# A batch's steps dealt out anew over five engines, and softmax's reductions folded

## The chip, the cores and the metric

One core of a Trainium2 chip runs the kernel; the others are idle. The time is the device time of one execution in microseconds. A core has TensorE (PE), VectorE (DVE), ScalarE (ACT) and GpSimd (POOL), each with a queue of its own that it works off in order, and SyncE (SP), which here only issues DMAs. Engines wait for each other through semaphores.

## What is computed

The input x is 4 batches of 1024 tokens with 128 channels, float32. Two blocks follow one another, each between two layer norms:

```python
x = x + layernorm(attention(layernorm(x)))
x = x + layernorm(experts(layernorm(x)))
```

Attention (8 heads of 16 channels) scores each token against 11 earlier positions: itself and those 1, 2, 4, ... 512 back. Over these 11 scores goes a softmax, whose weights sum the values at the same positions. Added to it are a causal convolution of the values over 7 taps per channel, and a linear attention (elu(q)+1, elu(k)+1) over all tokens. The sum goes through Wo, and attention adds its own input. The second block has 8 experts of 128 to 64 to 128 with gelu, of which a sigmoid gate keeps the best two per token, and a shared expert of the same size.

## The kernel before

It is a software pipeline written out by hand: each engine's program is a list of steps in a loop `for b in range(B + 1)`. In turn b the attention of batch b runs together with the experts of batch b-1, which has two units of 512 tokens, u0 = 2b-2 and u1 = 2b-1. `more` means that a batch b+1 follows, `ffn` that a batch b-1 exists. The turn ends with the keys, queries and values of batch b+1. Turn 0 has no experts, turn 4 has only experts. In the text batch b is the turn b.

The steps, in the order in which a batch needs them (lines of the profile):

- **Scores.** DVE multiplies queries with shifted keys in three groups of 4, 4 and 3 products (`products`, L957, L283), PE sums over each head's channels in three groups (`sum_heads`, L1330), ACT copies them (`scores`), PE turns them to token-major (`turn_scores`, L1260). `linear_state` on PE (L1311) and DVE (L975 to L981) makes fk^T v; the third score group waits for its `kv_ready`.
- **Softmax** on DVE: `softmax_logits` (L983) adds a mask, takes the maximum over the 12 slots and subtracts it; ACT takes exponentials (`exponentials`, L698); `softmax_weights` (L1001) sums them, takes the reciprocal (`rden`) and scales. The twelfth slot, masked out, is then given 1/z of the linear part, from `zden`. `weigh_low` (L1010) scales with it what PE made in `low` (L1348).
- **Terms.** For each of 8 tiles of 128 tokens DVE weighs the 11 shifted value tiles (`weigh`, L1032), PE sums them in PSUM by transposes (`sum_terms`, L1362), DVE adds the convolution (`add_conv`, L1052), PE applies Wo and adds the block's input (`output`, L1372). The shifted values `v_shift` are copies made by 18 DMAs of SP from token-major v (`shift_v`, L369 to L372).
- **Convolution.** ACT scales v by one tap at a time (`scale_taps`, L666), each into a home of its own (`tap_home`: convT, tapT0 to tapT2, then the buffers kexp and qexp, and tapT0 again). POOL adds them by six accumulating DMAs (`sum_taps_first`, `_second`, `_third`, L503); it waits for the landing of one before it issues the next of the same target. `key_parts` of the next batch waits for the last.
- **Layer norms.** ACT squares with a sum (`norm2`, `norm3_squares`, `norm4`), POOL takes the power -0.5 (`ln1` to `ln4`, L482 and L484), ACT or DVE applies it (`normalise1`, `normalise3`, `residual`, `finish`, `scale_outputs`).
- **Experts**, per unit: `turn_x3` (PE), `evacuate_x3` (ACT), `gate_logits` (PE: a matmul into the front bank C4, which holds logits and the shared expert's hidden part; ACT: its copy to `gate_shared`, and the exponential gexp), `turn_logits` (PE); 24 small dependent steps `gates` on DVE, each waiting for the one before; `gates_expert_major` (PE, ACT), `gate_rows`; `hidden` (PE matmuls, ACT gelu, 4 chunks); `spread_gates` (PE), `gate_hidden` (DVE, L1145); `experts_out` (PE, L1465, 4 tiles of 10 matmul records). DVE does u0's gates ahead of softmax_logits and u1's among the term tiles 0 to 3.
- **Fillers.** `keep_busy` (L1474) issues transposes of the identity into a free bank. Their result is not used. Before: 12 ahead of the third score group, 10 ahead of `turn_x3` of u0, 4 and 8 around u1's logits, per batch, and further ones in turns 0 and 4.

ACT needs another function table for gelu than for exp; changing costs an ACT_TABLE_LOAD.

The projections of batch b+1 stand on PE as `project_k` ahead of the terms, `project_q` at tile 1 and `project_v` at tile 5, before and after the change.

## Time and profile before

| | |
|---|---|
| median of 3 runs | 298.2 us (297.54 to 298.52) |
| the profiled execution's own time | 298.78 us |
| its span in the trace | 296.9 us |
| PE busy | 255.2 us, 86% |
| DVE busy | 233.1 us, 79% |
| ACT busy | 198.8 us, 67% |
| POOL busy | 87.1 us, 29% |
| chain that ended last | PE 53%, ACT 19%, DVE 16%, POOL 7% |
| mean granted clock of TensorE | 0.974 |

Busy time is the time in which at least one instruction of the engine runs; register, semaphore and DMA-issuing instructions aren't counted. The chain is followed back from the last instruction, at each step to what released it. The granted clock is 1.00 where TensorE runs at 2.4 GHz and 0.50 where it runs at 1.2.

### The profile page before, as it was taken

To read this page: it belongs to the slowest core of one execution; us is meant where nothing else is said; L and a number is where in the kernel's file an instruction comes from. 1 tells how busy PE (TensorE), PEld (TensorE's weight loads), DVE (VectorE), ACT (ScalarE), POOL (GpSimd) and SP (SyncE) were. 2 spreads that over 40 slices of the span, in tenths; PEclk is the share of its full clock that TensorE was granted. 3 is DMA by queue.
4 is the path that set the end of the run, shared out by engine and by line. 5 is a ranking of instruction groups with operands and counts; after the bars stand their busy time and mean duration, and the time that the engine had idled before them with its cause. 6 is when DMAs were issued, how large, how long until landed. Compare 5 with 4: busy or idle time off the path is not lost.

```text
span 296.9 us, 4821 instructions
## 1 busy us (share of the span) xinstructions
PE 255.2 (86%) x1665; PEld 180.1 (61%) x1665; DVE 233.1 (79%) x574; ACT 198.8 (67%) x461; POOL 87.1 (29%) x152
## 2 busy tenths in 40 slices
PE   5965987896599899989898899989898699699893
...
GB/s 198 128 45 243 227 191 191 95 0 111 234 243 201 153 44 2 141 0 162 242 235 223 162 2 35 35 26 221 238 220 219 97 2 71 2 1 1 0 14 94
DMA packets 24258, 35.27 MB, mean 119 GB/s; under 512 B 4053, under 2 KB 17198, under 8 KB 24234
## 3 DMA queue, kind: packets, MB, share of 16 engines
...
q0 software_dynamic: 3888, 13.37, 25.0%
...
q14 instruction: 11, 0.09, 0.1%
...
## 4 chain that ended last, share of the span: by engine, by line
PE 53%; ACT 19%; DVE 16%; POOL 7%; issue 4%; POOLq 0%; DVEq 0%; ACTq 0%
PE psH L1362 7%; PE psY L1465 6%; PE psA L1330 4%; PE psF L1427 4%; DVE prods L283 3%; PE psA L1268 3%; ACT xn L604 3%; PE psA L1260 3%; PE psG L1465 3%; PE psY L1311 3%; PE psA L1465 3%; DVE hid L1145 3%; POOL rstd L484 2%; PE psF L1402 2%; ACT xn L724 2%
## 5 line engine op out<-in xcount | busy, mean ns | idle before, releaser
L283 DVE TENSOR_TENSOR prods<-qT,kT 128x1024 f32<-128x1024 f32 (+1 forms) x48 | 50.4, 1106 | 2.8 <-POOL neg_half L447 2.8
L482 POOL TENSOR_SCALAR var<-ss 128x4 f32<-128x4 f32 (+1 forms) x25 | 12.5, 502 | 111.5 <-ACT squares L770 55.8
L1362 PE MATMUL psH<-ident,prods 128*128 128x128 f32 x324 | 40.0, 273 | 0.0
L1362 PEld LDWEIGHTS psH<-ident,prods 128*128 128x128 f32 x324 | 36.4, 141 | 2.3 <-issue 2.3
L1032 DVE TENSOR_TENSOR prods<-v_shift,prob 128x896 f32<-128x896 f32 x32 | 34.6, 1083 | 0.0
L484 POOL TENSOR_TENSOR rstd<-var,neg_half 128x4 f32<-128x4 f32 (+2 forms) x28 | 33.0, 1180 | 2.3
L1145 DVE TENSOR_TENSOR hid<-hid,psG 128x512 f32<-128x512 f32 x32 | 20.8, 682 | 15.8 <-PE psG L1451 15.2
L1427 PE MATMUL psF<-x3T,w 128*128 128x512 f32 x58 | 29.0, 610 | 0.4 <-ACT gexp L738 0.3
L1330 PE MATMUL psA<-prods,slot_sel 128*32 128x512 f32 x168 | 24.1, 624 | 4.1 <-DVE prods L283 4.1
L1032 DVE TENSOR_TENSOR prods<-v_tok,prob 128x128 f32<-128x128 f32 (+2 forms) x60 | 20.8, 371 | 1.9 <-PE psH L1362 1.9
L1465 PEld LDWEIGHTS psY<-w,hid 128*128 128x128 f32 x140 | 17.4, 206 | 5.7 <-DVE prods L1016 5.7
L1465 PE MATMUL psY<-w,hid 128*128 128x128 f32 x140 | 18.1, 292 | 3.2 <-DVE prods L1016 3.2
L503 POOL DMA_DIRECT2D convT<-tapT x9 | 8.1, 902 | 40.4 <-DMA convT<-tapT 22.4
L1474 PE MATMUL psG<-ident 128*128 128x128 f32 x126 | 17.1, 296 | 3.1 <-POOL ident L414 3.1
L1268 PE MATMUL psA<-xnT,wqkv 128*128 128x512 f32 x36 | 18.1, 631 | 1.5 <-ACT xnT L593 1.5
L746 ACT ACTIVATE hid<-psF,b1c 128x512 f32<-128x512 f32 x29 | 18.7, 684 | 0.7 <-PE psF L1427 0.5
L1474 PEld LDWEIGHTS psG<-ident 128*128 128x128 f32 x126 | 16.0, 154 | 5.2 <-POOL ident L414 3.1
L1427 PEld LDWEIGHTS psF<-x3T,w 128*128 128x128 f32 x58 | 9.7, 189 | 12.5 <-issue 8.5
L770 ACT ACTIVATE squares<-psY 128x128 f32<-128x128 f32 x14 | 3.7, 278 | 16.2 <-PE psY L1465 16.2
L1330 PEld LDWEIGHTS psA<-prods,slot_sel 128*32 128x32 f32 x168 | 5.2, 113 | 13.7 <-issue 11.4
L666 ACT ACTIVATE tapT<-vT,cw 128x1024 f32<-128x1024 f32 x12 | 13.1, 1139 | 0.0
L1359 PE MATMUL psH<-ident,prods 128*128 128x128 f32 x32 | 9.1, 285 | 3.5 <-DVE prods L1052 2.5
...
## 6 DMA issues: line engine op xcount, KB each, us to landing
...
convT<-tapT POOLq DMA_DIRECT2D x11, 512.0 KB, 5.0
x_res<-L_attn_x SPq DMA_DIRECT2D x4, 512.0 KB, 9.9
tapT<-tapT POOLq DMA_DIRECT2D x4, 512.0 KB, 10.1
...
x_in<-L_attn_x SPq DMA_DIRECT2D x3, 512.0 KB, 4.2
...
convT<-kexp POOLq DMA_DIRECT2D x3, 512.0 KB, 7.4
```

Of the source, the lines that this page charges most:

```text
L283: return eng.tensor_tensor(prods[:, QUADS * (s % 2) + q, t0:t1], qT[:, t0:t1], kT[:, PRE - off + t0:PRE - off + t1], ALU.mult)
L484: return nc.gpsimd.tensor_tensor(rstd[:, cols], var[:, cols], neg_half[:, cols], ALU.pow)
L666: nc.scalar.activation(tap_home(b, tap), vT[:, VPRE - tap:VPRE - tap + T], ACT.Copy, scale=cw[:, TAPS - 1 - tap:TAPS - tap]).then_inc(tap_ ...
L746: nc.scalar.activation(hid[:, c, half_cols(u)], hidden_bank(u, c), ACT.Gelu, bias=b1c[:, c:c + 1]).then_inc(hidden_free, 1)
L1032: return nc.vector.tensor_tensor(dst, src.rearrange("p m (h d) -> p m h d", d=HD), w, ALU.mult)
L1145: nc.vector.tensor_tensor(hid[:, c, cols], hid[:, c, cols], psG[:, c % 2, :], ALU.mult).then_inc(gated, 1)
L1268: pe.matmul(psA[:, half, :], wqkv[:, bass.ts(part, P)], xnT[(b + 1) % 2][:, bass.ts(half, HALF)], start=True, stop=True).then_inc(psA_full, 1)
L1330: ins = pe.matmul(psA[32 * q:32 * q + 32, half, :], ksum_sel[:] if low else slot_sel[:, s, :], fqT[:, cols] if low else prods[:, QUADS * ( ...
L1362: ins = pe.matmul(dst, terms[:, j % TERM_BUFS, m, :], ident[:], is_transpose=True, start=False, stop=(m == live[-1]))
L1427: pe.matmul(hidden_bank(u, c), w1[:, bass.ts(c, P)], x3T[:, half_cols(u)], start=True, stop=True).then_inc(hidden_full, 1)
L1465: ins = pe.matmul(output_tile(u, n), hid[:, c, bass.ts(j, P)], w2[:, c, :], start=(c == CH - 1), stop=(c == CH - 2))
L1474: pe.transpose(bank[:, bass.ts(k % TPH, P)], ident[:], ident[:])
```

## The change

- **Fold.** `over_terms` takes the place of both `tensor_reduce`: it halves the 12 slots to 6, these to 3, and combines those three in two steps, four chained tensor_tensor operations. `softmax_chain` counts 11 steps in place of 5. The reciprocal of zden is now taken in `weigh_low`, in place, and no longer stored in prob.
- **DVE order.** `stats` behind the second product group; `finish` and `residual(u1)` behind `linear_state`; two gate steps of u0 ride with the third group, two with `linear_state`; `weigh_low` and half of u0's `gate_hidden` ahead of `softmax_weights`; u1's gates ride with tiles 1 to 4, its `gate_hidden` at tiles 6 and 7.
- **Unit 2b's front.** `turn_x3`, `gate_logits` and their copies go from the start of turn b+1 to the end of turn b. On ACT the copy of C4 is split off as `evacuate_shared`.
- **Tap 6** has the home fkT and waits for the token-major fk in place of the first tap sum; taps 4 and 5 are scaled at the turn's start, tap 6 among u1's front.
- **POOL order.** `ln1`, `ln4`, the first tap sums (before: at the end of the turn before), `ln3(u1)`, the other tap sums; `ln2` of the second unit at the turn's end.
- **PE order.** `experts_out(u0)` is cut in three around u1's logits, `experts_out(u1)` in three around the token-major turns. The fillers of the steady turns are gone; the last attention turn has two of 10.

The diff, without its unchanged context where that says nothing ("..." stands for lines left out; indentation is cut per piece):

```diff
-FILL_SUM = 12
 FILL_FRONT = 5
-FILL_X3, FILL_C4, FILL_LOGITS = 10, 4, 8
+FILL_LAST = 10
...
-return (convT[b % 2], tapT[0], tapT[1], tapT[2], kexp, qexp, tapT[0])[tap][:]
+return (convT[b % 2], tapT[0], tapT[1], tapT[2], kexp, qexp, fkT)[tap][:]
...
-if ffn:
-    ln2(u1)
-if 2 <= b < B:
-    ln4(u0 - 1)
-if attn and b:
-    sum_taps_second(b)
-if more:
-    ln1(b + 1)
-if ffn and attn:
-    ln3(u1)
-if attn and b:
-    sum_taps_third(b)
-if ffn and attn:
-    ln4(u0)
-    add_residual(u0)
-if b == 0:
-    first_conv_sums()
 if attn:
+    if more:
+        ln1(b + 1)
+    if b >= 2:
+        ln4(u0 - 1)
+    if b:
+        sum_taps_first(b)
+        ln3(u1)
+        sum_taps_second(b)
+        sum_taps_third(b)
+        ln4(u0)
+        add_residual(u0)
+    else:
+        first_conv_sums()
     ln2(2 * b)
-if more:
-    sum_taps_first(b + 1)
-if attn:
     ln3(2 * b)
-if not attn:
+    ln2(2 * b + 1)
...
-act.wait_ge(sums_added, N_DMA * upto(b - 1, N_SUMS, 1))
+act.wait_ge(psA_full, filled(b, PSA_FK_TOK, 1))
...
-def gate_logits(u):
+def evacuate_shared(u):
     act.wait_ge(front_full, upto(u, N_FRONT, 2))
     copy(gate_shared[:, half_cols(u)], front(u, C4)).then_inc(front_free, 1)
+def gate_logits(u):
...
-    evacuate_x3(u0)
-if ffn:
     gate_logits(u0)
-if b:
-    scale_taps(b, range(5, TAPS))
-if ffn:
+    scale_taps(b, range(4, 6))
+    if more:
+        normalise1(b + 1, range(0, TPH))
     norm3_squares(u1)
-    hidden(u0, range(0, 2))
-if more and b:
-    normalise1(b + 1, range(0, TPH))
 scores(b)
 if b == 0:
     scale_first_taps(range(4, TAPS))
-if more and b:
-    normalise1(b + 1, range(TPH, NT))
 if ffn:
-    normalise3(u1)
+    if more:
+        normalise1(b + 1, range(TPH, NT))
+    hidden(u0, range(0, 2))
+    gates_expert_major(u0)
+    gate_rows(u0)
     hidden(u0, range(2, 4))
     shared_hidden(u0)
-    gates_expert_major(u0)
-    gate_rows(u0)
-    evacuate_x3(u1)
 exponentials(b)
-if ffn:
-    gate_logits(u1)
 if b == 0:
     normalise1(b + 1)
 if more:
     evacuate_x(b + 1)
+if ffn:
+    normalise3(u1)
+    evacuate_x3(u1)
+    scale_taps(b, range(6, TAPS))
+    evacuate_shared(u1)
+    gate_logits(u1)
+if more:
     evacuate_k(b + 1)
 if ffn:
     hidden(u1, range(0, 2))
-if ffn:
     norm4(u0)
 if more:
     evacuate_q(b + 1)
 if ffn:
     scale_outputs(u0)
-if ffn:
     hidden(u1, range(2, 4))
     shared_hidden(u1)
     gates_expert_major(u1)
 if more:
     key_parts(b + 1)
     query_parts(b + 1)
-norm2(2 * b)
-if not more:
+    norm2(2 * b)
+    evacuate_v(b + 1)
+    scale_taps(b + 1, range(0, 1))
+    norm3_squares(2 * b)
+    norm2(2 * b + 1)
+    normalise3(2 * b)
+    token_major_v(b + 1)
+    evacuate_x3(2 * b)
+    scale_taps(b + 1, range(1, 2))
+    token_major_fk(b + 1)
+    evacuate_shared(2 * b)
+    scale_taps(b + 1, range(2, 3))
+    if ffn:
+        norm4(u1)
+    scale_taps(b + 1, range(3, 4))
+else:
+    norm2(2 * b)
     norm3_squares(2 * b)
     nc.scalar.activation(table_load[:], neg_half[:, 0:1], ACT.Exp)
     norm2(2 * b + 1)
     normalise3(2 * b)
-if more:
-    evacuate_v(b + 1)
-    scale_taps(b + 1, range(0, 4))
-if more:
-    token_major_v(b + 1)
-    token_major_fk(b + 1)
-    norm3_squares(2 * b)
-    norm2(2 * b + 1)
-    scale_taps(b + 1, range(4, 5))
-    normalise3(2 * b)
-    if ffn:
-        norm4(u1)
...
+def over_terms(op, into):
+    tt, n = nc.vector.tensor_tensor, NM // 4
+    softmax_chain(tt(folded[:], prob[:, :, 0:NM // 2, :], prob[:, :, NM // 2:NM, :], op))
+    softmax_chain(tt(folded[:, :, 0:n, :], folded[:, :, 0:n, :], folded[:, :, n:2 * n, :], op))
+    softmax_chain(tt(into[:], folded[:, :, 0, :], folded[:, :, 1, :], op))
+    softmax_chain(tt(into[:], into[:], folded[:, :, 2, :], op))
...
-softmax_chain(nc.vector.tensor_reduce(top[:], prob[:].rearrange("p j m h -> p j h m"), AX_X, ALU.max))
+over_terms(ALU.max, top)
 nc.vector.tensor_tensor(prob[:], prob[:], top[:].unsqueeze(2).to_broadcast([P, NT, NM, HEADS]),
...
-    softmax_chain(nc.vector.tensor_reduce(den[:], prob[:].rearrange("p j m h -> p j h m"), AX_X, ALU.add))
-    softmax_chain(nc.vector.reciprocal(rden[:], den[:]))
+    over_terms(ALU.add, den)
+    softmax_chain(nc.vector.reciprocal(den[:], den[:]))
     softmax_chain(nc.vector.tensor_tensor(prob[:], prob[:],
-                                          rden[:].unsqueeze(2).to_broadcast([P, NT, NM, HEADS]),
+                                          den[:].unsqueeze(2).to_broadcast([P, NT, NM, HEADS]),
                                           ALU.mult))
-    softmax_chain(nc.vector.reciprocal(prob[:, :, M_LOW, :], zden[:]))
 def weigh_low(b):
+    softmax_chain(nc.vector.reciprocal(zden[:], zden[:]))
     dve.wait_ge(low_ready, upto(b, 1, 1))
     for half, src in enumerate((psH, psY)):
         tiles = slice(half * TPH, (half + 1) * TPH)
-        w = prob[:, tiles, M_LOW, :].unsqueeze(3).to_broadcast([P, TPH, HEADS, HD])
+        w = zden[:, tiles, :].unsqueeze(3).to_broadcast([P, TPH, HEADS, HD])
         ins = nc.vector.tensor_tensor(low_terms[:, tiles].rearrange("p j (h d) -> p j h d", d=HD),
...
+if u % 2 == 0 or u == 2 * B - 1:
...
         products(b, 1)
         key_features(0)
     query_features(b)
-    if more and b:
-        stats(b + 1)
     if b:
         products(b, 1)
-def gate_step_of(u, first):
-    def beside(n):
-        if attn and ffn:
-            gates(u, (first + n,))
-    return beside
-if attn and not more:
-    products(b, 2)
-if attn and b >= 2:
-    finish(u0 - 1)
-if ffn:
-    residual(u1)
-if more:
-    products(b, 2, gate_step_of(u0, 0))
-if attn:
-    linear_state(b, gate_step_of(u0, 3 if more else 0))
+        if more:
+            stats(b + 1)
+    products(b, 2, range(0, 1))
+    products(b, 2, range(1, 3), gate_step_of(u0, 0))
+    linear_state(b, gate_step_of(u0, 2))
     if b == 0:
         stats(b + 1)
         centre_weights()
         dve.wait_ge(consts_ready, 2)
+    if b >= 2:
+        finish(u0 - 1)
     if ffn:
-        gates(u0, range(5 if more else 2, 24))
+        residual(u1)
+        gates(u0, range(4, 24))
     softmax_logits(b)
     if ffn:
-        gate_hidden(u0, range(0, 4))
+        gate_hidden(u0, range(0, 2))
+    weigh_low(b)
+    if ffn:
+        gate_hidden(u0, range(2, 4))
     softmax_weights(b)
-    weigh_low(b)
     for j in range(NT):
         def two_gate_steps(n):
-            if ffn and j < TPH:
-                gates(u1, range(2 * (3 * j + n), 2 * (3 * j + n + 1)))
+            if ffn and 1 <= j <= TPH:
+                gates(u1, range(2 * (3 * (j - 1) + n), 2 * (3 * (j - 1) + n + 1)))
         weigh(b, j, two_gate_steps)
         if ffn:
-            if j in (5, 7):
-                gate_hidden(u1, range(j - 5, j - 3))
+            if j in (6, 7):
+                gate_hidden(u1, range(2 * (j - 6), 2 * (j - 5)))
...
-if 0 < u < 2 * B - 2 and u % 2 == 0:
-    keep_busy(FILL_X3, front(u, X3))
...
-if u < 2 * B - 2 and u % 2:
-    keep_busy(FILL_C4, front(u, C4))
...
-if u < 2 * B - 2 and u % 2:
-    keep_busy(FILL_LOGITS, front(u, LOGITS))
...
-    turn_x3(u0)
-    gate_logits(u0)
+    turn_logits(u0)
 linear_state(b, b == 0)
-if ffn:
-    turn_logits(u0)
 if b:
     sum_heads(b, 1)
+else:
+    keep_busy(FIRST_FILL_SUM, psG[:, 1, :])
+sum_heads(b, 2)
 if ffn:
     hidden(u0, range(0, 2))
-keep_busy(FILL_SUM if b else FIRST_FILL_SUM, psG[:, 1, :])
-sum_heads(b, 2)
-if ffn:
-    hidden(u0, (2,))
 turn_scores(b)
 if ffn:
-    hidden(u0, (3,))
+    gates_expert_major(u0)
 low(b)
 if b == 0:
     pe.wait_ge(w_centred, 1)
+    keep_busy(FIRST_FILL_X, psG[:, 1, :])
+if ffn:
+    hidden(u0, (2,))
+    spread_gates(u0, range(0, 2))
+    hidden(u0, (3,))
+if more:
+    turn_x(b + 1)
+if not more:
+    pe.wait_ge(scores_read, 2 * B)
+    keep_busy(FILL_LAST, psA[:, 0, :])
+if ffn:
+    spread_gates(u0, range(2, 4))
+if more:
+    project_k(b + 1)
+else:
...
 if ffn:
     turn_x3(u1)
-    gates_expert_major(u0)
-if b == 0:
-    keep_busy(FIRST_FILL_X, psG[:, 1, :])
-if more:
-    turn_x(b + 1)
-if ffn:
-    spread_gates(u0, range(0, 2))
+    experts_out(u0, (0,))
     gate_logits(u1)
-    spread_gates(u0, range(2, 4))
+    experts_out(u0, (1,))
     turn_logits(u1)
-if more:
-    project_k(b + 1)
-if ffn:
+    experts_out(u0, range(2, TPH))
     hidden(u1, range(0, 2))
 if b == 0:
     project_q(b + 1)
-if ffn:
-    experts_out(u0)
-if b == 0:
...
-            spread_gates(u1, range(2 * (j - 5), 2 * (j - 4)))
-    if more:
-        if j == 1 and b:
-            project_q(b + 1)
-        if j == 5:
-            project_v(b + 1)
+        if j in (5, 7):
+            spread_gates(u1, range(j - 5, j - 3))
+    if more and j == 1 and b:
+        project_q(b + 1)
+    if more and j == 5:
+        project_v(b + 1)
     sum_terms(b, j)
     if j == TPH:
         output(b, 0)
 output(b, 1)
 if more:
+    if ffn:
+        experts_out(u1, range(0, 2))
     token_major_v(b + 1)
+    turn_x3(2 * b)
+    if ffn:
+        experts_out(u1, range(2, 3))
     token_major_fk(b + 1)
+    gate_logits(2 * b)
 if ffn:
-    experts_out(u1, range(TPH if more else TPH - 1))
+    experts_out(u1, range(TPH - 1, TPH) if more else range(TPH - 1))
```

## Rows read from the trace of the kernel before

**Rows 1.** Busy time by stretch, halves A and B of batches 1, 2, 3 (in turn).

Columns: stretch, its length, busy time (and instructions) of PE, weight loads, DVE, ACT, POOL, granted clock of TensorE, DMA share, GB/s.

```profile
69.22:94.06 24.84, 19.16 (x121) 11.12 (x120) 21.02 (x61) 18.20 (x50) 9.91 (x16) 0.93 0.91 218
94.06:133.22 39.16, 36.27 (x234) 26.10 (x233) 33.01 (x75) 31.30 (x62) 6.64 (x7) 1.00 0.35 76
133.22:158.21 24.99, 22.92 (x171) 15.39 (x170) 22.12 (x65) 19.73 (x59) 14.79 (x19) 1.00 0.87 209
158.21:197.37 39.16, 36.28 (x234) 26.11 (x233) 33.03 (x75) 31.29 (x62) 5.95 (x7) 1.00 0.34 74
197.37:221.19 23.82, 22.64 (x171) 15.44 (x170) 20.18 (x49) 18.76 (x56) 12.48 (x14) 1.00 0.88 205
221.19:258.03 36.84, 30.51 (x205) 23.42 (x203) 31.88 (x72) 17.13 (x46) 5.62 (x7) 0.95 0.39 88
```

**Rows 2.** Groups by line and shape, PE, batch 2 (134.34 to 198.49): filler transposes.

```profile
L1474 PE MATMUL psF<-ident 128*128 128x128 f32 x22 | 3.1, 280 | 0.0
...
L1474 PE MATMUL psG<-ident 128*128 128x128 f32 x12 | 1.5, 272 | 0.0
```

**Rows 3.** Waits of DVE, batch 2: half A, then half B.

```profile
DVE y_out L1155 <- POOL rstd L484: 1.2, 1, 1.2
...
DVE hid L1145 <- PE psG L1451: 4.2, 3, 1.7
DVE prods L1052 <- PE psH L1362: 1.2, 1, 1.2
```

**Rows 4.** Timeline of DVE, batch 2: logits start, weighing starts, first add_conv.

```profile
158.21 0.22 DVE L988 TENSOR_SCALAR zden<-psA 128x64 f32<-128x64 f32 x1 [0.88 <-PE psA L1260]
...
171.84 0.28 DVE L1032 TENSOR_TENSOR prods<-v_tok,prob 128x128 f32<-128x128 f32 x1
...
184.66 0.69 DVE L1052 TENSOR_TENSOR prods<-psH,convT 128x512 f32<-128x512 f32 x1 [1.25 <-PE psH L1362]
```

**Rows 5.** Groups by line and shape, DVE, batch 2.

```profile
L283 DVE TENSOR_TENSOR prods<-qT,kT 128x1024 f32<-128x1024 f32 x11 | 12.9, 1213 | 0.0
...
L1003 DVE TENSOR_REDUCE den<-prob 128x64 f32<-128x768 f32 x1 | 1.5, 1520 | 0.0
...
L1005 DVE TENSOR_TENSOR prob<-prob,rden 128x768 f32<-128x768 f32 x1 | 1.0, 957 | 0.0
...
L990 DVE TENSOR_TENSOR prob<-psA,mask 128x384 f32<-128x384 f32 x2 | 1.0, 547 | 0.0
...
L1096 DVE TENSOR_TENSOR gtmp<-gtmp,first_pref 128x32 f32<-128x32 f32 x2 | 0.4, 192 | 0.1
```

**Rows 6.** Groups by line and shape, ACT, batch 2: softmax's exponentials.

```profile
L698 ACT ACT_TABLE_LOAD x1 | 1.3, 1283 | 0.0
...
L698 ACT ACTIVATE prob<-prob 128x768 f32<-128x768 f32 x1 | 0.8, 844 | 0.0
```

**Rows 7.** Busy time by stretch, batch 3, around the start of experts_out.

```profile
232.00:233.00 1.00, 0.00 (x0) 0.00 (x0) 0.93 (x3) 0.24 (x1) 0.00 (x0) 1.00 1.02 205
...
235.00:236.00 1.00, 1.00 (x7) 1.00 (x7) 0.97 (x3) 0.00 (x0) 0.00 (x0) 0.50 0.00 0
```

**Rows 8.** Timeline of PE: experts_out of the first unit, batches 2 and 3.

```profile
171.98 4.73 PE L1465 MATMUL psY<-w,hid 128*128 128x128 f32 x40 [0.22 <-DVE prods L1016]
...
234.12 6.19 PE L1465 MATMUL psY<-w,hid 128*128 128x128 f32 x40 [2.78 <-DVE prods L1016]
```

**Rows 9.** Timeline of POOL, batch 2: tap sums issued.

```profile
133.90 0.93 POOL L503 DMA_DIRECT2D convT<-tapT  x1 [3.56 <-ACT tapT L666]
...
149.72 0.93 POOL L503 DMA_DIRECT2D convT<-kexp  x1 [3.38 <-ACT qexp L666]
...
157.52 0.93 POOL L503 DMA_DIRECT2D convT<-tapT  x1 [1.01 <-DMA convT<-kexp]
...
166.37 0.86 POOL L503 DMA_DIRECT2D convT<-tapT  x1 [7.92 <-DMA convT<-tapT]
```

**Rows 10.** Page, DMA issues: KB each, median us from issue to landing.

```profile
convT<-tapT POOLq DMA_DIRECT2D x11, 512.0 KB, 5.0
```

More of the change, by code:

```diff
@@ L955, in query_features, with products @@
                                                op1=ALU.add).then_inc(fq_ready, 1)
-            def products(b, s, beside=lambda n: None):
+            def products(b, s, some=range(QUADS), beside=lambda n: None):
                 if s == 0 and b:
@@ L969, in products @@
                     dve.wait_ge(psA_free, first_count(PSA_Q, 1))
-                for n, q in enumerate(mine):
+                for n, q in enumerate(mine[some.start:some.stop]):
                     ins = product(nc.vector, s, q, HALF if b == 0 and s == 0 else 0, T)
@@ L1164, in _, with gate_step_of, beside @@
                 u0, u1 = 2 * b - 2, 2 * b - 1
+                def gate_step_of(u, first):
+                    def beside(n):
+                        if ffn and n >= 0:
+                            gates(u, (first + n,))
+                    return beside
                 if attn:
```

11 lines of the change are left out of this document (7 added, 4 removed).

## The prediction

> **What bounds the kernel now.** I read three views. First the page's busy shares and the chain that ended last: TensorE (PE) is busy 86% of the span, VectorE (DVE) 79%, ScalarE (ACT) 67%, and the chain changes engines all the time. No engine is full, so handovers are the price. Second, DVE's own list of instructions, from which I took two marks in each batch: k, where `key_features` ends and the products start, and L, where `softmax_logits` starts. They cut batches 1, 2 and 3 into halves A (k to L) and B (L to the next k; in batch 3 to the end of the last `add_conv`). In [rows 1] the reader sees each half's length and DVE's busy time in it. The six halves are 188.8 us, and DVE works 161.2 us of them: at most 27.6 us can be won without taking work from DVE. PE is busy 167.8 us, but part of that is filler: 22 and 12 transposes of `keep_busy` in one batch, 280 and 272 ns each as records overlap, at a start-to-start of about 0.11 us, so some 4 us a batch [rows 2]. Without it PE has about 156 us of work, less than DVE. So the engine to watch is DVE, and the question for every part is which wait of DVE goes and which comes. Third, DVE's waits in batch 2: in A it waits 1.2 us for `ln4` in `finish` [rows 3] and 0.9 us for the turned scores, at L itself [rows 4]; in B 4.2 us for the spread gates and 1.2 us for the terms' sums [rows 3]. In the other batches the sets are alike.
>
> **Half A, part by part.**
> - ACT and PE now turn x3, project C4 and copy it (`turn_x3`, `gate_logits`, `evacuate_x3`, `evacuate_shared` of unit 2b) at the end of the batch before, among `experts_out(u1)`. It is the same work; what leaves A is a ping-pong between PE and ACT ahead of the logits of unit u0. It costs something on the other side: `token_major_v` on ACT now stands behind `normalise3(2b)`, and that behind POOL's `ln3`; v_tok and fk_tok come some 2 and 3 us later after k than before. They feed the v_shift copies, `linear_state` and the first score sums. I cost this at nothing, because DVE has eight products (1.2 us each, the next starting a little before one ends [rows 5]) and the query features to do in that time.
> - `finish(u0-1)` and `residual(u1)` go from ahead of the third product group to behind `linear_state`. POOL now takes `ln1(b+1)` before `ln4`; `ln1` waits for `stats`, which moved behind the second products. I get `ln4` ready about when DVE arrives, and keep 0.2 us of wait in batch 2. The 0.9 to 2.8 us wait for the turned scores goes: the scores are summed while DVE does finish, residual and 20 gate steps (each one starts 0.224 us after the last).
> - So DVE runs A nearly without a wait. Its busy time [rows 1] plus the gaps between the dependent gate steps (about 0.035 each, 0.8 in all) gives 21.0 + 1.1 = 22.1, 22.1 + 1.1 = 23.2, and 20.2 + 0.7 = 20.9 us, against 24.8, 25.0 and 23.8: 7.4 us less.
>
> **Half B, part by part.**
> - The folds: a reduction takes 1.52 us, a tensor_tensor of 768 elements 0.957, of 384 0.547, of 32 0.192 [rows 5]. A fold is 384, 192, 64 and 64 elements; by the line through these rows 0.55 + 0.35 + 2 x 0.22, and three gaps of 0.035, so 1.45 us. The bounds are 1.3 (all gaps overlapped) and 1.6. It wins 0.1 us each, 0.8 in the whole run. This goes against what one would read from the page: the Trainium skill (VectorE: DVE Perf Modes, "Rules for kernel authors") says of chained operations to keep their number small. By that rule alone a fold, four operations for one, would lose about 0.5 us against a reduction that ran at the pace of the 768-element row, or 4 us over the eight folds. The trace's reduction does not run at that pace, and I go by the row.
> - The reciprocal for the linear part and `weigh_low` (0.55 + 1.2 us) and two of the four `gate_hidden` go ahead of `softmax_weights`, into the time in which ACT makes the exponentials. ACT has to do the hidden layers first, load the table (1.28 us) and take 0.84 us for the exponentials [rows 6]: by my count prob is there 7.2 us after L, and DVE arrives at 7.9. `softmax_weights` ends at 11.0, where before weighing began 13.6 us after L [rows 4]. 2.6 us won.
> - Given back: `normalise3(u1)` and x3T of u1 now come after the exponentials, and the logits of u1 pass PE between `experts_out` tiles. They reach gexp 13.7 us after L. The gate steps, though moved from tiles 0-3 to 1-4, want it at 12.4: a new wait of 1.3 us in batches 1 and 2 (in batch 3, without x and k to copy, almost none).
> - The waits for the sums before `add_conv(b, 0)` (1.2 us) go, as PE is ahead there; of the waits for u1's spread gates I keep 0.75 us, and 0.7 us before `residual(2b)`, whose rstd comes from POOL late.
> - B in sum: 33.0 + 1.3 + 0.75 + 0.7 + 0.75 (gaps) = 36.5 us twice, and 31.9 + 1.3 = 33.2 in batch 3, against 39.2, 39.2, 36.8: 9.0 us less.
>
> Batch 0 ends where PE's term sums end, which the folds don't touch, and the tail after the last batch has its order kept: both nothing. If batch 0's cover failed it would be the DVE wins of about 1 us, downward.
>
> **The clock.** The fillers go, and PE now stands idle in four places of a batch: about 3 us before the third score group (it needs kv, behind 3 products of 1.2 us and the statistics), 2 before `low`, 2.7 before `project_k`, 1 before `turn_x3`. The trace prices that: with PE idle for 2.8 us, its granted clock goes to 0.50 (1.2 GHz of 2.4) [rows 7], and the 40 matmuls of `experts_out` then take 6.19 us where they take 4.73 at the full clock [rows 8]: 1.46 us. The bounds for a batch are 0 (it falls where DVE is the later one, as with the third score group, 2 us ahead of need) and 4 x 1.46 = 5.8. I take one such stretch on the path in each of three batches, as in batch 3 of the old trace: 4.4 us. The Trainium skill (TensorE: Matmul & The Clock Gate, Part 1) says the same: idle TensorE falls to the lower level and has to earn the higher one by activity. [...]
>
> **Sum.** The profiled execution took 298.8 us, which is 0.6 above the median of 298.2. 298.8 - 7.4 - 9.0 + 4.4 = 286.8, and 0.6 less for the median: 286.2 us.
>
> **Rivals.**
> 1. *No clock cost.* The gaps of PE are shorter than I count, or fall in DVE's cover. Then 281.8. For: in batch 2 of the old trace the clock is 1.00 throughout. Against: the fillers that held it so are gone.
> 2. *The clock costs more.* One to two more stretches per batch on the path (before `low` and `project_k`): 3 x 1.46 = 4.4 to 3 x 2 x 1.46 = 8.8 more, so 291 to 295; the page's rule above falls on the lower end. For it: between L - 7 and L + 10 PE has work for half the time only. Against: DVE is the later one at most of these places.
> 3. *The tap sums come late, and it is slower.* Before, the chain of accumulating DMAs is issued 0.7, 16.5, 24.3 and 33.2 us after k, [rows 9], and its last, 5.0 us to land [rows 10], is there 13 us before `add_conv` at 51.4 [rows 4]. Now the first goes out only behind `ln1` and `ln4`, 16 us after k, and `add_conv` comes at 47 (44.5 in batch 3). With links of 8.9, 7.8, 5 and 5 us it lands at 43, in time. With all four links at 8.9 us (the longest in [rows 9], while the v_shift copies run) it lands at 52, and POOL, which sits in those waits, also holds `ln4(u0)` and y_out's residual back. Price 5 + 5 + 7.5 = 17.5, so 304. It decides at a mean link of 7.7 us. Against: v_shift is alone on the queues before, so it should be out of the way by the third link.
> 4. *Another engine takes over* (ACT is busy 51 us a batch, DVE 55): what DVE no longer waits for in [rows 3] comes back as waits for ACT's longer queue ahead of gexp and v_tok. If all of 16.4 but the clock cost is given back, it is no change, 298; POOL's moves alone would not do it.
>
> **Chances.** Forecast (284 to 290) 0.52; rival 1 0.13; rival 2 0.20; rival 3 0.07; rival 4 0.05; and 0.03 for clock and waits together beyond the old time. This kernel's measurement can tell about 0.3% (0.9 us) from no change. Faster 0.86, same 0.05, slower 0.09. The range leaves out rival 3 and most of 4 and reaches down to rival 1 less the fold's lower bound: 281 to 295.5.
>
> **What would show it.** The halves of batches 1 to 3 at about 22, 23, 21 and 36.5, 36.5, 33 us; no wait of DVE for the turned scores; `softmax_weights` starting without a wait for prob; a new wait of 1 to 2 us for gexp at tile 1; fold chains of 1.45 us; granted clock below 0.97 in half A or early B; POOL's waits on tap sums ended before 45 us after k. A DVE wait on the sums in `add_conv`, or an A half above 24 us, would prove me wrong.

## The result and the profile after

The changed kernel takes 303.2 us, median of 4 runs (301.88 to 305.14), beside 297.9 for the kernel before in as many runs: a ratio of 1.0191 (95% interval 1.0145 to 1.0238). It is slower by 5.4 us, where 286.2 was forecast (range 281 to 295.5). The profiled execution took 302.4 us; its span is 300.6 us, and the mean granted clock 0.943 against 0.974. The ratios further down are to the kernel before, run in the same session as the experiment; its medians there were 296.8 to 297.5 us. In experiments 4 and 9 some runs lay over 1.5% above the fastest of their kernel, and the times and ratios given are those of the others.

The page of the changed kernel, busy times and the engines of the chain that ended last:

```profile
PE 252.2 (84%) x1593; PEld 174.9 (58%) x1593; DVE 231.0 (77%) x598; ACT 198.0 (66%) x461; POOL 94.7 (32%) x152
PE 48%; DVE 22%; ACT 12%; DMA 8%; POOL 5%; issue 3%; POOLq 0%; DVEq 0%; ACTq 0%
```

The engines work slightly less than before (PE 3 us, DVE 2, ACT 1), except POOL (7.6 more). So the 5 us are idle time, and the busy shares don't say where it is. The halves do. They are those of [rows 1] in the changed kernel, A1, B1, A2, B2, A3, B3, with the same marks k and L:

```profile
core 0: us, PE busy (x) PEld busy (x) DVE busy (x) ACT busy (x) POOL busy (x), PEclk, DMA share, GB/s
69.52:91.94 22.42, 16.22 (x108) 8.29 (x107) 20.99 (x61) 16.00 (x41) 10.77 (x12) 0.92 0.65 180
91.94:134.17 42.23, 37.25 (x224) 26.31 (x223) 32.71 (x79) 33.30 (x70) 8.47 (x10) 0.96 0.49 103
134.17:159.43 25.26, 19.98 (x146) 13.02 (x144) 22.09 (x65) 18.70 (x51) 14.65 (x17) 0.95 0.67 181
159.43:203.19 43.76, 38.88 (x224) 27.85 (x225) 32.77 (x80) 32.08 (x68) 8.43 (x10) 0.91 0.40 82
203.19:224.98 21.79, 19.14 (x146) 12.43 (x144) 20.02 (x49) 17.15 (x45) 11.68 (x13) 1.00 0.64 161
224.98:261.65 36.67, 32.23 (x215) 25.15 (x215) 31.52 (x79) 19.93 (x51) 7.32 (x8) 0.95 0.57 126
```

The A halves are 69.5 us in sum, 4.2 less than before. The B halves are 122.7, 7.5 more: 3.1 in batch 1, 4.6 in batch 2, nothing in batch 3. So the gain came, smaller than thought, and the loss sits in B of the two batches that also project the next batch's q, k and v. The tail is 38.95 us, as before (38.9). All halves are read from one profiled execution of each kernel.

DVE's waits in B1, read from its timeline (start, duration, instruction, and in brackets the idle time before it with what ended it; "..." stands for lines left out):

```profile
91.94 0.23 DVE L993 TENSOR_SCALAR zden<-psA 128x64 f32<-128x64 f32 x1 [0.74 <-PE psA L1263]
...
96.08 1.28 DVE L1150 TENSOR_TENSOR hid<-hid,psG 128x512 f32<-128x512 f32 x2 [0.49 <-PE psG L1448]
...
100.97 0.56 DVE L983 TENSOR_TENSOR folded<-prob 128x384 f32<-128x384 f32 x1 [0.63 <-ACT prob L691]
...
109.28 0.18 DVE L1091 TENSOR_SCALAR gtmp<-gexp 128x32 f32<-128x32 f32 x1 [3.73 <-ACT gexp L733]
...
121.11 0.69 DVE L1057 TENSOR_TENSOR prods<-psH,convT 128x512 f32<-128x512 f32 x1 [1.73 <-PE psH L1365]
...
130.20 1.29 DVE L1150 TENSOR_TENSOR hid<-hid,psG 128x512 f32<-128x512 f32 x2 [2.11 <-PE psG L1448]
```

Behind L (whose own 0.74 belongs to A) these are 0.5 + 0.6 + 3.7 + 1.7 + 2.1 = 8.7 us, where I had 1.3 + 0.75 and 0.7 ahead of `residual(2b)`, which did not wait here. The wait for gexp is three times what I gave it, and the wait for the term sums ahead of `add_conv`, which I let go, is longer than before. B2 has the same list (2.03, 0.62, 3.73, 1.67, 2.11). B3 has 3.04 for gexp, where I had almost none, and none at `add_conv`.

What releases them is in PE's timeline of the same stretch, from the end of `spread_gates` to the sums of tile 3:

```profile
98.11 0.60 PE L1448 MATMUL psG<-gT,gate_sel 24*128 24x512 bf16 x2
101.47 3.06 PE L1271 MATMUL psA<-xnT,wqkv 128*128 128x512 f32 x4 [2.75 <-ACT xnT L586]
104.33 1.06 PE L1394 MATMUL psF<-ident,xn 128*128 128x128 f32 x4
105.18 1.51 PE L1462 MATMUL psY<-w,hid 128*128 128x128 f32 x10
106.53 1.02 PE L1401 MATMUL psF<-x3T,w 128*128 128x512 f32 x2
107.39 1.28 PE L1462 MATMUL psY<-w,hid 128*128 128x128 f32 x10
108.59 0.41 PE L1406 MATMUL psF<-ident,gate_shared 8*128 8x8 f32 x4
108.94 2.50 PE L1462 MATMUL psY<-w,hid 128*128 128x128 f32 x20
111.27 1.88 PE L1424 MATMUL psF<-x3T,w 128*128 128x512 f32 x4
112.99 0.27 PE L1362 MATMUL psH<-ident,prods 128*128 128x128 f32 x1
113.10 1.04 PE L1365 MATMUL psH<-ident,prods 128*128 128x128 f32 x8
113.97 1.88 PE L1271 MATMUL psA<-xnT,wqkv 128*128 128x512 f32 x4
...
119.81 1.25 PE L1365 MATMUL psH<-ident,prods 128*128 128x128 f32 x10
```

The reader is to see one bracket at the top and none after it; the lines left out have none either. PE waits 2.75 us for xnT, which ACT copies only behind the exponentials; then it works without a pause for 19.6 us, and at its end (121.06) `add_conv` is let go. In this stretch DVE isn't the bound: PE is, by its queue. In the kernel before (L is at 94.06) the front of u1, lines L1393, L1402 and L1409, stands ahead of `project_k`:

```profile
97.01 0.66 PE L1393 MATMUL psF<-ident,xn 128*128 128x128 f32 x4 [0.35 <-ACT hid L746]
...
100.08 1.12 PE L1402 MATMUL psF<-x3T,w 128*128 128x512 f32 x2
...
102.73 0.41 PE L1409 MATMUL psF<-ident,gate_shared 8*128 8x8 f32 x4
103.91 1.98 PE L1268 MATMUL psA<-xnT,wqkv 128*128 128x512 f32 x4 [0.78 <-ACT xnT L593]
105.73 1.88 PE L1427 MATMUL psF<-x3T,w 128*128 128x512 f32 x4
107.83 4.73 PE L1465 MATMUL psY<-w,hid 128*128 128x128 f32 x40 [0.22 <-DVE prods L1016]
```

The same marks, side by side:

| batch 1, us | before | after |
|---|---|---|
| L to the start of `project_k` | 9.85 | 9.53 |
| `project_k` to `add_conv` of the first half | 16.60 | 19.64 |
| `add_conv` to the next k | 12.71 | 13.06 |
| B | 39.16 | 42.23 |

The middle line is the loss of B1. By the starts of PE's instructions it is 0.85 + 0.86 + 0.35 = 2.06 us for x3, C4 and logits of u1, which used to come ahead of `project_k` and now stand behind it; 1.04 because `project_k` takes 2.86 us and not 1.82; 0.31 in `experts_out`; less 0.38 of small gaps closed: 3.03. The slow `project_k` is the clock; a table of stretches inside B1 shows it:

```profile
102.00:104.00 2.00, 2.00 (x4) 0.71 (x3) 1.90 (x4) 1.43 (x4) 0.00 (x0) 0.56 0.12 23
104.00:106.00 2.00, 2.00 (x11) 1.67 (x10) 1.51 (x4) 0.58 (x2) 0.00 (x0) 0.59 0.00 0
106.00:108.00 2.00, 2.00 (x15) 1.52 (x14) 0.00 (x0) 1.47 (x3) 0.65 (x1) 1.00 0.00 0
```

After the 2.75 us of idling the granted clock is at 0.56 to 0.59, near the 1.2 GHz level, for the matmuls of `project_k` and until 106, then full. So the turned x3 and the first tile of experts behind `project_k` run slow too, and part of their share above is the clock; experiment 1 separates the two.

In batch 2 the middle line is 19.64 again and the last 13.06; the first is 11.06, since `low` runs slow there, ACT's last gelus wait for the hidden chunks behind it, and the exponentials and xnT come 1.5 us later than in batch 1. That is B2's 1.5 us more. In batch 3, without `project_k`, PE isn't full: it waits 2.44 us for `normalise3(u1)` on ACT, which stands behind the exponentials, then runs `turn_x3` and most of a tile of experts at a clock of 0.50, and DVE waits 3.04 us for gexp.

### The profile page after: what moved, and what is told of

Same layout as the page of the kernel before. It is cut to its first block, busy times and chain, and to the rows that moved or that the text cites. A ratio compares the mean times of both kernels' runs of the same rounds, so it can differ in the third digit from the quotient of the medians.

```text
span 300.6 us, 4732 instructions
## 1 busy us (share of the span) xinstructions
PE 252.2 (84%) x1593; PEld 174.9 (58%) x1593; DVE 231.0 (77%) x598; ACT 198.0 (66%) x461; POOL 94.7 (32%) x152
## 4 chain that ended last, share of the span: by engine, by line
PE 48%; DVE 22%; ACT 12%; DMA 8%; POOL 5%; issue 3%; POOLq 0%; DVEq 0%; ACTq 0%
DVE prods L282 10%; PE psH L1365 9%; PE psF L1424 6%; PE psY L1462 6%; PE psA L1271 5%; POOL rstd L483 3%; PE psA L1462 3%; DMA gate_shared<-x3T 3%; DMA gate_shared<-hid 2%; PE psG L1448 2%; PE psA L1333 2%; DVE prods L1057 2%; ACT xn L717 2%; ACT squares L710 2%; DMA convT<-gate_shared 2%
## 5 line engine op out<-in xcount | busy, mean ns | idle before, releaser
L483 POOL TENSOR_TENSOR rstd<-var,neg_half 128x4 f32<-128x4 f32 (+2 forms) x28 | 40.4, 1442 | 2.3
L1365 PE MATMUL psH<-ident,prods 128*128 128x128 f32 x324 | 39.9, 273 | 0.0
L481 POOL TENSOR_SCALAR var<-ss 128x4 f32<-128x4 f32 (+1 forms) x25 | 9.0, 358 | 92.0 <-ACT squares L703 34.6
L1333 PE MATMUL psA<-prods,slot_sel 128*32 128x512 f32 x168 | 26.0, 666 | 8.1 <-DVE kv L977 5.7
L1271 PE MATMUL psA<-xnT,wqkv 128*128 128x512 f32 x36 | 22.1, 751 | 5.5 <-ACT xnT L586 5.5
L1037 DVE TENSOR_TENSOR prods<-v_tok,prob 128x128 f32<-128x128 f32 (+2 forms) x60 | 20.9, 371 | 4.8 <-PE psH L1365 4.7
L597 ACT ACTIVATE xn<-x_in,nmr,rstd 128x128 f32<-128x128 f32 x24 | 9.8, 483 | 10.9 <-POOL nmr L499 10.9
L1271 PEld LDWEIGHTS psA<-xnT,wqkv 128*128 128x128 f32 x36 | 7.6, 230 | 14.4 <-ACT xnT L586 8.0
L1471 PE MATMUL psG<-ident 128*128 128x128 f32 x90 | 12.3, 300 | 3.1 <-POOL ident L413 3.1
L1471 PEld LDWEIGHTS psG<-ident 128*128 128x128 f32 x90 | 11.7, 158 | 3.6 <-POOL ident L413 3.1
L710 ACT ACTIVATE squares<-x,neg_mean 128x128 f32<-128x128 f32 x24 | 9.3, 389 | 6.0 <-DVE x L1068 6.0
```

Of the source, the lines that this page charges most:

```text
L483: return nc.gpsimd.tensor_tensor(rstd[:, cols], var[:, cols], neg_half[:, cols], ALU.pow)
L710: last = nc.scalar.activation(squares[:, j, :], x2_of(u)[:, j, :], ACT.Square, bias=neg_mean[:, u // 2 % 3, j:j + 1], accum_out=ss3[:, j:j ...
L1037: return nc.vector.tensor_tensor(dst, src.rearrange("p m (h d) -> p m h d", d=HD), w, ALU.mult)
L1271: pe.matmul(psA[:, half, :], wqkv[:, bass.ts(part, P)], xnT[(b + 1) % 2][:, bass.ts(half, HALF)], start=True, stop=True).then_inc(psA_full, 1)
L1333: ins = pe.matmul(psA[32 * q:32 * q + 32, half, :], ksum_sel[:] if low else slot_sel[:, s, :], fqT[:, cols] if low else prods[:, QUADS * ( ...
L1365: ins = pe.matmul(dst, terms[:, j % TERM_BUFS, m, :], ident[:], is_transpose=True, start=False, stop=(m == live[-1]))
```

## The experiments

Two theories stood after the result. **Order**: PE's queue behind the late `project_k` is full, so each instruction placed there pushes `add_conv`, whatever the clock. **Clock**: the fillers that went held the granted clock, and their loss is the loss. Each kernel is the changed one with the edit shown, unless said otherwise.

**1. Fillers ahead of `project_k`.**

```diff
+if more and ffn:
+    pe.wait_ge(hidden_free, upto(u1, N_HIDDEN, -1))
+    keep_busy(26, front(u1, X3))
 if more:
     project_k(b + 1)
```

> The changed kernel with 26 filler transposes ahead of project_k in batches 1 and 2, where TensorE stood idle for 2.75 us. Clock theory (the lost fillers are the whole loss): the granted clock stays at 1.00 over project_k and turn_x3, the four matmul records of project_k take 1.98 us in place of 3.06 and 3.67, half B of batches 1 and 2 falls from 42.2 and 43.8 us to about 37, and the kernel comes to about 291. Order theory (TensorE has too much left to do after the exponentials): the clock is mended just the same, but half B only falls by the 1.9 and 2.5 us that the slow stretch cost, to 40.3 and 41.3, and the kernel comes to 298.5 to 299.5.

Measured: 300.9 us, ratio to before 1.0101 (1.0034 to 1.0168). B1 is 40.52 at clock 1.00 and B2 42.40. The wait for gexp falls from 3.73 to 2.36; that for the sums stays at 1.73. The middle line of the table is 18.20 us in B1: of its 3.0 us of loss 1.4 was the clock, and 1.6 is left. By the ratios the clock ahead of `project_k` is worth some 0.9%, 2.7 us, though the two intervals overlap; by B1 and B2 it is 3.1 of the 7.7 us that they lost. The rest has another cause. B3, which the edit doesn't touch, was 38.24 us in this profile and 36.67 in the one of the changed kernel, at a clock of 0.91 and 0.95: a half of a single profile can move by that much.

**2. Fillers ahead of the third score group**, 34 of them, as many as the kernel before had in a whole batch.

```diff
+if b:
+    keep_busy(34, psG[:, 1, :])
 sum_heads(b, 2)
```

> The changed kernel with 34 filler transposes ahead of the third score group in batches 1 to 3. Clock theory: clock 1.00 over the third score group (batch 1) and over turn_scores and low (batch 2); half A of batch 1 shorter by its 0.7 us wait for the turned scores, half B of batch 2 shorter by 1.5 us (the 2.0 us wait for the first spread gates), 301 in all. Order theory: the same here, since it only denies that this is most of the loss; if TensorE is late for another reason, the fillers themselves (0.11 us each) may be in its way and cost up to 1 us a batch.

Measured: 304.3 us, 1.022 (1.0154 to 1.0286), no gain. The clock of A2 is 1.00 where it was 0.95, and A2 is 25.25 us as before it; A1 is 22.17, A3 longer (23.40). PE's slow stretch before the third group lies beside DVE's work and costs nothing. The 1.5 us that I expected in B2 didn't come (43.58): PE waits again ahead of `low`, and `low` still runs slow. B1 is 43.80, 1.6 more: the 2.75 us gap ahead of `project_k` is there as before, and `project_k` takes 3.78 us.

**3. The front of u1 ahead of `project_k`,** on ACT its normalise and x3 ahead of the exponentials, as before the change. The lines put in are shown; the same calls go from where they stood, and `experts_out(u0)` is in one piece again.

```diff
     shared_hidden(u0)
+    normalise3(u1)
+    evacuate_x3(u1)
 exponentials(b)
+if ffn:
+    evacuate_shared(u1)
+    gate_logits(u1)
...
+if ffn:
+    turn_x3(u1)
+    gate_logits(u1)
+    turn_logits(u1)
 if more:
     project_k(b + 1)
+if ffn:
+    experts_out(u0)
```

> The changed kernel with the front of unit u1 (normalise3, turn_x3, the C4 matmul, the turned logits and their copies) put back ahead of project_k, on ScalarE ahead of the exponentials. Order theory: gexp is there by about 11 us after L in place of 17 to 19, the 3.7 us wait of VectorE for it is gone, the exponentials come about 2.2 us later, half B of batches 1 and 2 comes to 40 or less and that of batch 3 to 35, the kernel to 296 to 299. Clock theory: the work that is now in the idle stretch keeps the clock up as well, but the exponentials that come 2.2 us later put the same time on VectorE's path, so no more than the 1.9 and 2.5 us of the slow stretch come back: 299.

Measured: 310.9 us, 1.0434 (1.0357 to 1.0511): a miss, and the most instructive one. From PE's timeline in B1 (L is at 93.91):

```profile
102.24 0.63 PE L1395 MATMUL psF<-ident,xn 128*128 128x128 f32 x4 [1.88 <-ACT xn L717]
103.64 1.10 PE L1402 MATMUL psF<-x3T,w 128*128 128x512 f32 x2 [0.78 <-ACT x3T L586]
106.19 0.41 PE L1407 MATMUL psF<-ident,gate_shared 8*128 8x8 f32 x4 [1.45 <-ACT gate_shared L586]
107.38 2.95 PE L1272 MATMUL psA<-xnT,wqkv 128*128 128x512 f32 x4 [0.78 <-ACT xnT L586]
```

Four brackets in a row: PE plays ping-pong with ACT while the bulk waits behind it. `project_k` starts 13.5 us after L and not 9.5, and takes 2.95 us. The wait for gexp is gone, as both theories had it, but the exponentials are later (DVE waits 3.7 for prob), and `add_conv` waits 4.2. B1 is 44.3 us. Not the place of the front alone, but how late the full part of PE's queue starts, sets the end of B.

**4. `project_v` behind the last term sum** (it stood at tile 5).

```diff
-if more and j == 5:
-    project_v(b + 1)
...
+if more:
+    project_v(b + 1)
 output(b, 1)
```

> The changed kernel with project_v taken out from among the terms (tile 5) and put between the last term sum and the second output. Order theory: VectorE's wait for u1's last two spread gates falls from 2.1 us to about 0.4 in batches 1 and 2, and half B by about 1.7 us each, 300 in all; the later v comes to ScalarE about when it wants it. Clock theory: half B ends with TensorE's sums in either case, no change, 303.

Measured: 300.9 us, the mean of two runs (299.0 and 302.8), 1.0109 (0.9992 to 1.0227), unclear. The 2.11 us wait for the last spread gates is 0.35 now, and DVE waits in the next batch instead, for the first score sums:

```profile
128.13 1.29 DVE L1150 TENSOR_TENSOR hid<-hid,psG 128x512 f32<-128x512 f32 x2 [0.35 <-PE psG L1448]
...
147.58 2.37 DVE L282 TENSOR_TENSOR prods<-qT,kT 128x1024 f32<-128x1024 f32 x2 [2.67 <-PE psA L1333]
```

B1 is 41.93, 0.3 us less, with the wait for gexp 0.7 longer; A2 is 25.60, 0.3 more, for the new wait stands in place of the 2.36 us for `ln4`. By this profile the wait for the spread gates was PE's work too, and what is taken from its place returns elsewhere; the time of the kernel, with two runs, is too uncertain to add to that.

**5. Two tiles of `experts_out(u0)` ahead of `project_k`,** in the time PE stands idle. (In the last attention turn the fillers stay ahead of them.)

```diff
+if ffn:
+    experts_out(u0, range(0, 2))
 if more:
     project_k(b + 1)
 if ffn:
     turn_x3(u1)
-    experts_out(u0, (0,))
+    experts_out(u0, (2,))
     gate_logits(u1)
-    experts_out(u0, (1,))
+    experts_out(u0, (3,))
     turn_logits(u1)
-    experts_out(u0, range(2, TPH))
```

> The changed kernel with two tiles of experts_out(u0) ahead of project_k, the other two among u1's front, so that 2.2 us of real work stands where TensorE was idle for 2.75 us. Order theory: project_k starts up to 0.5 us later, what is behind it is 2.2 us shorter and runs at the full clock; half B of batches 1 and 2 falls by 3.5 to 4.5 us, to 38 to 40, the kernel to 294 to 297. Clock theory: only the slow stretch (1.9 and 2.5 us) comes back, as with the fillers: 299 to 301.

Measured: 296.1 us, 0.9956 (0.9921 to 0.9991): within what the order theory expected, and some 7 us less than the changed kernel from one permutation. From PE's timeline (L is at 91.96):

```profile
99.16 2.80 PE L1462 MATMUL psY<-w,hid 128*128 128x128 f32 x20 [0.49 <-DVE prods L1021]
101.80 1.88 PE L1271 MATMUL psA<-xnT,wqkv 128*128 128x512 f32 x4
103.53 0.63 PE L1394 MATMUL psF<-ident,xn 128*128 128x128 f32 x4
...
116.17 1.25 PE L1365 MATMUL psH<-ident,prods 128*128 128x128 f32 x10
```

The bracket of 2.75 is 0.49, and `project_k` still starts 9.84 us after L. From there to the end of the sums of tile 3 (117.42) it is 15.6 us in place of 19.6: 2.5 us of experts are gone from it, 1.1 because `project_k` runs at full clock, 0.3 in the rest. `add_conv` no longer waits; gexp costs 2.36:

```profile
91.96:130.84 38.88, 35.94 (x224) 25.49 (x223) 32.53 (x79) 32.91 (x70) 7.72 (x10) 1.00 0.53 112
156.09:196.62 40.53, 37.58 (x224) 27.29 (x225) 32.58 (x80) 31.76 (x68) 7.72 (x10) 0.95 0.46 94
218.41:253.23 34.82, 30.81 (x215) 23.62 (x215) 31.44 (x79) 19.82 (x51) 7.02 (x8) 1.00 0.60 130
```

These are B1, B2 and B3: 3.4, 3.2 and 1.9 us less than after. Experiment 1 filled the same gap in batches 1 and 2 with work that is of no use and won 3.1 us of B1 and B2, where this permutation wins 6.6: the other 3.5 us (1.6 and 1.9) I put down to the order. B3, at a clock of 1.00 and not 0.95, has no like among the filler runs, so clock and order aren't separated there.

**6. Hidden chunks 0 and 1 of u0 earlier,** ahead of `sum_heads(b, 2)` on PE and of `normalise1` on ACT, to have the exponentials sooner. PE's part of the edit:

```diff
+hidden(u0, range(0, 2))
 sum_heads(b, 2)
-hidden(u0, range(0, 2))
 turn_scores(b)
```

> The changed kernel with the first two hidden chunks of u0 ahead of the third score group on TensorE, and their gelu (and its table load) ahead of normalise1 on ScalarE, where both engines waited (3.8 and 5.8 us). Order theory: the exponentials come about 2 us earlier after L, project_k starts at L + 7.5 in place of L + 9.5, VectorE reaches softmax_weights without a wait, and half B falls by about 2 us in all three batches, 297. Clock theory: the work in TensorE's gap holds the clock as well, and TensorE's later gap gets shorter than 2.75 us, so the slow stretch goes: 298 too, but only if the granted clock in half B rises to 1.00; if the clock stays low and the time falls all the same, order is what counts.

Measured: 303.3 us, 1.0215 (1.0158 to 1.0271), nothing won. ACT's timeline says why:

```profile
92.41 0.63 ACT L586 ACTIVATE hid<-gT 24x512 f32<-24x512 bf16 x1
95.52 0.69 ACT L741 ACTIVATE hid<-psF,b1c 128x512 f32<-128x512 f32 x1 [2.48 <-PE psF L1424]
97.05 0.69 ACT L741 ACTIVATE hid<-psF,b1c 128x512 f32<-128x512 f32 x1 [0.84 <-PE psF L1424]
```

ACT was free sooner and waited 2.5 us for chunk 2, which PE makes behind `low`. The exponentials came at L + 8.5 (after: 8.2).

**7. The kernel before without its steady fillers** (34 per batch).

```diff
-keep_busy(FILL_SUM if b else FIRST_FILL_SUM, psG[:, 1, :])
+if b == 0:
+    keep_busy(FIRST_FILL_SUM, psG[:, 1, :])
...
-keep_busy(FILL_X3, front(u, X3))
...
-keep_busy(FILL_C4, front(u, C4))
...
-keep_busy(FILL_LOGITS, front(u, LOGITS))
```

> The kernel before without its fillers of batches 1 to 3 (12, 10, 4 and 8 transposes a batch), everything else left. Clock theory: the fillers are what kept the clock up, so it falls in each batch, and the kernel goes to 302 or more. Order theory: in the old order there is real work in most of TensorE's gaps, the clock falls once a batch at most, and the kernel stays within 2 us of before, either way.

Measured: 298.5 us, 1.0052 (1.0023 to 1.008). In the old order the fillers are worth 0.5%, 1.6 us; I had charged 4.4 us for their loss.

**8. Experiments 5 and 6 together, and `ln4` ahead of `ln1` on POOL.**

```diff
-if more:
-    ln1(b + 1)
 if b >= 2:
     ln4(u0 - 1)
+if more:
+    ln1(b + 1)
```

> experts_first and hidden_early together, and ln4 ahead of ln1 on GpSimd (VectorE waited 2.4 us for it in batch 2). Order theory: the gains add up in part, half A of batch 2 at 23, halves B at 37 to 38 and 35, the kernel at 289 to 292, faster than before. Clock theory: no better than experts_first alone, since the clock can be mended only once: 296 to 299.

Measured: 294.7 us, 0.9906 (0.9866 to 0.9947): faster than both kernels, the best that was run, and between the two expectations. Its windows of A2 and B3:

```profile
130.28:153.14 22.86, 19.21 (x146) 12.34 (x144) 22.04 (x64) 20.14 (x53) 14.62 (x16) 1.00 0.64 175
215.13:253.19 38.06, 34.05 (x215) 26.76 (x215) 31.46 (x79) 19.71 (x50) 7.29 (x9) 0.91 0.56 119
```

A2 is 22.9 us where it was 25.3: the 2.36 us wait for `ln4` is gone. B3 is 3.2 us longer than in experiment 5, at a clock of 0.91 and with 3.2 us more of PE busy; this part of the gain is given back in that profile, and I have not found out what would keep it.

**9. The fold alone,** on the kernel before.

```diff
-softmax_chain(nc.vector.tensor_reduce(top[:], ...
+over_terms(ALU.max, top)
...
-    softmax_chain(nc.vector.tensor_reduce(den[:], ...
+    over_terms(ALU.add, den)
```

> The kernel before with both reductions of softmax replaced by the four chained operations of the change (den scaled in place), nothing else. By the trace of the changed kernel a fold takes 1.5 us (0.56 + 0.36 + 0.22 + 0.22 and gaps), a reduction 1.52 to 1.56. Both theories: no change that can be measured, 297 to 298; if the fold were the hidden cost it would be 1 to 4 us slower.

Measured: 296.4 us, 0.9991 (0.9942 to 1.004), and every half within 0.05 us of before. DVE is busy 0.33 us less in each B, without the gaps between the four operations; nothing comes of it.

**10. All hidden chunks of u0, and the shared one, ahead of `normalise1` (ACT); on PE the chunks ahead of `turn_scores`.** PE's part of the edit:

```diff
+hidden(u0, range(0, 2))
 sum_heads(b, 2)
-hidden(u0, range(0, 2))
+hidden(u0, range(2, 4))
 turn_scores(b)
...
-    hidden(u0, (2,))
     spread_gates(u0, range(0, 2))
-    hidden(u0, (3,))
```

> The changed kernel with all four hidden chunks of u0 and the shared one ahead: on TensorE the first two ahead of the third score group, the other two behind it, ahead of turn_scores; on ScalarE all of them ahead of normalise1. Where hidden_early only moved ScalarE's wait to the third chunk, here nothing of the hidden layers is left after L. Order theory: the exponentials come at L + 4.5 to 5.5 in place of L + 8.1, project_k starts at L + 6 in place of L + 9.5, half B of batches 1 and 2 falls to about 39 and 40, of batch 3 to 35, and the kernel comes to 293 to 296. Clock theory: this takes 1.7 us of work from the stretch after L, so TensorE's gap there stays or grows, the clock falls as before, 299 or more.

Measured: 298.1 us, 1.0027 (0.9992 to 1.0062), between the two expectations. B is 37.3, 37.2 and 32.4 us, the shortest so far, since `project_k` starts at L + 6.1. A pays for it, 27.4, 27.8 and 26.0 us: ACT copies the scores behind the gelus, and PE's `turn_scores` waits for it.

```profile
93.54 1.97 PE L1262 MATMUL psA<-ident,prods 128*128 128x128 f32 x8 [5.21 <-ACT prods L586]
```

**11. The same with `ln4` ahead of `ln1`, and the last `spread_gates` of u1 at tile 6** in place of 7.

```diff
-if j in (5, 7):
-    spread_gates(u1, range(j - 5, j - 3))
+if j in (5, 6):
+    spread_gates(u1, range(2 * (j - 5), 2 * (j - 4)))
```

> hidden4, with ln4 ahead of ln1 on GpSimd, and u1's last two spread gates at tile 6 in place of 7. Order theory: half A of batch 2 falls by the 2.4 us wait of finish, the 2.1 us wait for the last spread gates falls to about 1, so 3 to 4 us below hidden4. Clock theory: only the ln4 wait, 2 us below.

Measured: 296.6 us, 0.9963 (0.9932 to 0.9994), 1.5 us below experiment 10, where the order theory had 3 to 4 and the clock theory 2. The wait for the last spread gates is 0.80 where it was 2.11, and B1 36.0. A2 is unchanged at 27.75: the wait in `finish` is gone, that for the turned scores grew from 2.42 to 4.86. Here the swap of experiment 8 wins nothing, because another wait ends later.

**12. The same with the experts of experiment 5.**

> hidden4_swap with two tiles of experts_out(u0) ahead of project_k, as in experts_first. Order theory: the gap that they filled is gone in hidden4, and they wait there for VectorE's gate_hidden; so the two changes do not add up, and this is as fast as hidden4_swap within 1.5 us, or slower. Clock theory: they fill TensorE as before and win another 3 us.

Measured: 305.4 us, 1.0253 (1.0195 to 1.031). The permutation that won 7 us loses 9 here:

```profile
103.34 3.99 PE L1461 MATMUL psY<-w,hid 128*128 128x128 f32 x20 [1.39 <-DVE prods L1020]
107.17 1.88 PE L1270 MATMUL psA<-xnT,wqkv 128*128 128x512 f32 x4
```

The gap it used is not there: xnT is ready early. The experts wait 1.39 us for DVE's `weigh_low`, which frees their bank, so they now hold `project_k` back until 11.5 us after L, and run at a low clock (3.99 us against 2.80). gexp is waited for 4.2 us in batch 1, 4.7 in batch 2.

## Why the prediction was wrong, step by step

- **The step that failed** is in half B: "The waits for the sums before `add_conv(b, 0)` (1.2 us) go, as PE is ahead there", and with it gexp 13.7 us after L. I took from [rows 1] that PE has less work than DVE over all six halves and didn't add up PE's queue in the one stretch where it is full: the prediction has no sum of it, and gives the 2.06 us of u1's front, now behind `project_k`, no place in it. What the runs showed in its place: start to start `project_k`, `project_q` and each pair of hidden chunks take 1.7 to 1.8 us at the full clock, and the stretch was 16.6 us long already in the kernel before. DVE read gexp at L + 17.3, a wait of 3.7 and not 1.3 us. Of the 3.6 us by which it came later, 1.8 were there when the exponentials ended (below), 1.0 is the slow `project_k`, and 0.8 is left for the queue from there to the logits. The sums' wait became 1.7 and not 0; the last spread gates, behind `project_v` and now at tile 7, 2.1 and not 0.75. Experiments 3, 5 and 12 show in batches 1 and 2 that the place and the start of PE's full stretch set the end of B. In batch 3 it is another path: PE waits for ACT's `normalise3(u1)` behind the exponentials, and the wait for gexp, where I had almost none, was 3.0.
- **By how much.** Half B was 42.2, 43.8 and 36.7 us against 36.5, 36.5 and 33.2, 16.5 us over; A was 3.3 over; both contain the clock, for which I had set 4.4 apart. That is 15.4 of the 17 us by which I missed; the rest is mostly that the profiled execution lay above the median before, and below it after.
- **Half A.** 22.4, 25.3 and 21.8 against 22.1, 23.2 and 20.9. The wait for the turned scores went, as I said (0.74 us is left in batch 1). In batch 2 the term of 0.2 us for `ln4` was 2.4: `ln1`, put ahead of it on POOL, took 4.9 us for its four operations on 128x8, where they took 3.0 before. Experiment 8 takes exactly that away. In batch 3 a wait of 0.98 us for the first score sums is the term that I put at nothing.
- **ACT ahead of the weights.** prob was ready at L + 9.0 in batch 1 (I had 7.2): ACT came to the first gelu's table load 0.6 us after L and had one wait of 0.6 us, for a hidden chunk that PE makes around `low`; the rest is its own list up to the exponentials. In batch 2 it waited 2.5 and 0.9 us for these chunks. DVE had a wait of 0.6 where I had none. `softmax_weights` ended at L + 12.1, not 11.0.
- **The fold.** 1.50 us from the start of its first to the start of the next instruction (93.13 to 94.63), against 1.45 forecast; the two reductions of batch 1 before took 1.58 and 1.55 by the same measure. Its worth for the run was forecast at 0.8 us and is not to be seen; the interval of experiment 9 is too wide to tell 0.8 from nothing, but its halves are those of before. The Trainium skill's advice to keep chained operations few (VectorE: DVE Perf Modes, "Rules for kernel authors"), taken alone, would have made it a loss; the trace doesn't bear that out for this reduction.
- **The clock.** The kind of event was right: in batch 1 the clock falls before the third score group, where DVE covers it (experiment 2), in batch 2 before the turned scores (0.50 from 158 to 162, over `low`), and in both before `project_k`, where nothing covers it. Its price was 2.7 us by experiment 1 and 1.6 in the old order by experiment 7, against 4.4. The Trainium skill's rule that idling lowers the clock and activity raises it (TensorE: Matmul & The Clock Gate, Part 1) gets the kind of event right; the section makes the fall depend on how long TensorE was idle, so it doesn't by itself give the 291 us at which rival 2 puts it. A3 kept 1.00. What stays open is batch 2, where `low` runs slow as well (2.08 + 1.84 us against 1.16 + 1.06 in batch 1) and B2 is 1.5 us longer than B1; no run had fillers right ahead of `low` in the changed order.
- **Rival 3** (tap sums too late) didn't happen: `add_conv` never waits for them in these batches.
- **Rival 4** is the nearest of the four, with mostly the wrong engine: what DVE no longer waited for came back as other waits, and more than all of it, but in batches 1 and 2 by PE's queue. What came, clock and waits together beyond the old time, had 0.03, and a slower kernel 0.09. Two of my own signs of being wrong appeared: a wait on the sums in `add_conv`, and a half A above 24 us.
